# Scores of the last attention on 32-row tiles of four row groups, with unread full-array products in front of side products and value sums

## The chip, the cores and the metric

The kernel runs on one core of a Trainium2 chip. The metric is the device time of one launch in microseconds (us), smaller is better. The core has TensorE (PE in the profile, its weight loads PEld), VectorE (DVE), ScalarE (ACT), GpSimd (POOL) and SyncE (SP), which only starts transfers here. TensorE writes to PSUM, eight banks of 128 partitions by 512 fp32 numbers.

## The reference

Four layers follow each other on an input of 2 x 1024 tokens of width 128. Each normalises `x`, computes an attention `s` and a gate `g`, and adds `s * g`. The change lies in the attention of the last one (`L3_attn`): 16 heads of width 8, causal, on both batch halves.

```python
y = (jnp.einsum('bse,ef->bsf', x, W1) + b1).reshape(B, S, 16, -1).transpose(0, 2, 1, 3)
q, k, v = jnp.split(y, 3, axis=-1)
w = jnp.einsum('bhqd,bhkd->bhqk', q, k) / dk          # dk = 8 ** 0.5
w = jax.nn.softmax(w * mask - 1e10 * (1.0 - mask), axis=-1)   # mask is lower triangular
attn = jnp.einsum('bhqk,bhkd->bhqd', w, v)
return jnp.einsum('bse,ef->bsf', attn.transpose(0, 2, 1, 3).reshape(B, S, E), W2) + b2
```

Its gate is a small quantised product with a low-rank part (`L3_ffn`), worked off beside the first heads.

## The kernel before

Class `Small` does this attention (`kind == 3`; `kind == 1` is the windowed attention of the second layer, which the change leaves as it is). `Lead` (normalisation, gate, values) runs in its first four heads.

*Layout.* Two batch halves of 16 heads make 32 heads `x`. Four heads with the same `n = x // 4` form a quad; head `hh = x % 4` of a quad holds 32 of the 128 partitions: three groups of eight rows with high and low parts of Q and K (the splitting makes up for the fp32r format), and in row 24 of the 32 the row maximum, negated, on Q's side against a one on K's side. Q of a quad lies in `QS[n % 3]` (128 x 1024). K is spread out: `KH[n % 3][hh]` holds the 32 rows of head `hh` and zeros in the other 96, so that a product over all 128 rows gives the scores of one head. ScalarE writes the copies for heads 0 and 2 (`spread`, L2114), GpSimd those for 1 and 3 (`spread_odd`, L1902), each 128 x 512 from `hm`, which holds the projected K.

*Steps.* The order of work is written out: `steps()` goes through head slots `x` of 14 steps `j`. In each step every engine issues what falls due there, in its own queue:
- `row(x, j)`: scores with queries on the partitions (L2007), 12 tiles of at most 512 columns a head (`rparts`). A query block of over 512 keys has two tiles, the first one (`first`) unmasked. VectorE reduces a first tile with one instruction (L2319) into `P2`, and any other with the causal mask added (L2323) into `MM`. After the twelfth one small instruction joins both parts (L2328, event `("both", x)`).
- `col(y, m)`: the scores again with keys on the partitions (L2028), 12 tiles (`cparts`), of the head that is `lag = 63` steps behind (four heads and a half). They contain the maximum through row 24 of Q. ScalarE takes the exp into `ET` (L2135), two buffers.
- `sums`: products of the values with `ET` (L2053), 128-row by 32-column tiles in four column groups, 32 matmuls and then 40, of head `x - 6`, at steps `AV_AT = (0, 4)`. They wait for GpSimd's `cut_off` (L1912), which zeroes the diagonals. ScalarE copies two heads' sums out (`take_out`, L2141) at step 6.
- `misc`: side units at steps 1, 4, 7. `project` makes 512 columns of Q or K of the next quad: three matmuls (L205 to L207), ScalarE's masked copy `hm` (L2102), VectorE's combination (L2235 for Q, L2238 for K). `max` turns the maxima (four transposes, L148) and VectorE adds them into Q (L2251). `give` turns the finished sums back. All use bank 7, one after another.

*Banks and waits.* Row scores go round banks 0 to 2, column scores round 3 to 5. `bank_free` makes TensorE wait until the reader has done with the tile three before. In a step TensorE issues first the column scores, then the row scores, then sums, then a side unit; all queues work strictly in that order. VectorE handles row tile, then side unit. `bc`, `mk` (the mask in bf16, 128 x 512: 384 columns of zeros and the causal block) and the projection weights are set up by `SmallWeights`. SyncE issues nothing in this stage between its loads and the three stores of the result.

The instruction order of TensorE and its waits for a bank:

```python
if m in self.at and 0 <= y < self.NH:
    col(y, self.at[m])
if j in self.at and x < self.NH:
    row(x, self.at[j])
if j in self.AV_AT and 0 <= x - 6 < self.NH:
    sums(x - 6, self.AV_AT.index(j))
if (x, j) in self.misc:
    side(self.misc[x, j])
```

## Time and profile before

| what | value |
|---|---|
| median of 3 runs | 1697.86 us (1697.16 to 1700.54) |
| profiled execution | 1706.63 us |
| its span | 1704.9 us |
| mean granted clock of TensorE | 0.952 |
| last attention | from about 1355 us to the end |

The page gives each engine's busy time and the costliest groups of instructions. The trace answers by stretch: a window of 39.1 us holds one quad of the steady part, in which every head slot has row scores, column scores and sums. The share of busy time of an engine does not say that it sets the pace: the view of waits says who was late for whom, and the view in order of time shows where in a head that happens.

### The profile page before, as it was taken

The page shows a single profiled execution, that of the slowest core. Times are in us where ns is not written, and L with a number is a line of the kernel's source. Part 1 is how long each engine was busy: PE and PEld are TensorE (multiplying, and loading weights), DVE is VectorE, ACT ScalarE, POOL GpSimd, SP SyncE. Part 2 cuts the span into 40 slices and gives each one's busy share as a digit, 9 for nine tenths or more (in the row PEclk, how much of TensorE's full clock was granted, in tenths as well). Part 3 has the DMA queues.
Part 4 walks back from the last instruction along what each step waited for, and adds up shares of the span by engine and source line. Part 5 has one row for each costly group of instructions (what it writes and reads, how often), then busy time and mean ns, then how long its engine had stood idle before and what let it go on. Part 6 is the DMA issues. An engine that isn't in the chain of part 4 may idle for free. (4 is left out here: it accounts for less than half of the span.)

```text
span 1704.9 us, 29946 instructions
## 1 busy us (share of the span) xinstructions
PE 1490.4 (87%) x11248; PEld 1197.3 (70%) x11248; DVE 1260.4 (74%) x2770; ACT 1089.9 (64%) x2122; POOL 857.1 (50%) x798
## 2 busy tenths in 40 slices
PE   6999999999999999899848888845999379998997
PEld 4788887888788887687737676834788256666675
DVE  6999999999999999435461677589433887777772
ACT  4888888888888888455445565632444456666665
POOL 4556576667666666720363744624666632233211
PEclk9999999999999999999779999957999699999999
DMA  3656666656666565300044000040465200000000
GB/s 94 124 103 115 106 120 100 120 108 114 115 108 103 99 105 106 87 1 1 18 137 129 26 2 2 2 133 1 112 148 109 64 1 1 2 2 2 2 2 26
DMA packets 334417, 117.09 MB, mean 69 GB/s; under 512 B 281008, under 2 KB 326096, under 8 KB 334144
## 3 DMA queue, kind: packets, MB, share of 16 engines
q1 hardware_dynamic: 323664, 101.54, 29.2%
q0 software_dynamic: 8496, 12.59, 3.4%
q8 instruction: 89, 1.46, 0.4%
q10 hardware_dynamic: 2112, 1.05, 0.2%
q14 instruction: 56, 0.46, 0.1%
HBM read 37.53 MB, written 10.49 MB: 28 GB/s over the span
## 5 line engine op out<-in xcount | busy, mean ns | idle before, releaser
L2135 ACT ACTIVATE ET_a<-PS 128x256 f32<-128x256 f32 (+2 forms) x512 | 220.5, 499 | 114.8 <-PE PS L2028 72.9
L771 POOL TENSOR_TENSOR dl<-XN,dh 128x1024 f16<-128x1024 f32 x86 | 184.9, 2150 | 155.2 <-DVE D L743 79.7
L205 PE MATMUL PS<-xh,yh 128*128 128x512 f32 x512 | 215.5, 421 | 6.6 <-ACT XNT L608 3.8
L206 PE MATMUL PS<-xl,yh 128*128 128x512 f32 x512 | 204.0, 398 | 0.0
L207 PE MATMUL PS<-xh,yl 128*128 128x512 f32 x512 | 202.8, 396 | 0.0
L608 ACT ACTIVATE G<-PS,nm 128x1024 f32<-128x1024 f32 x128 | 143.0, 1117 | 53.4 <-DVE nm L693 37.9
L608 ACT ACTIVATE XNT<-PS,nm 128x1024 f32<-128x1024 f32 x128 | 143.1, 1118 | 52.3 <-DVE nm L693 41.0
L687 DVE TENSOR_REDUCE nm<-PS 128x1 f32<-128x1024 f32 x128 | 156.6, 1223 | 15.7 <-PE PS L207 13.8
L689 DVE TENSOR_REDUCE nm<-PS 128x1 f32<-128x1024 f32 x128 | 156.0, 1219 | 4.7 <-PE PS L207 1.0
L205 PE MATMUL PS<-dth,xnh 128*128 128x256 f16 x512 | 141.0, 275 | 12.0 <-DVE zl L697 12.0
L2323 DVE CUSTOM_DVE_ANT_0 PS<-PS,mk 128x256 f32<-128x256 f32 (+3 forms) x256 | 128.2, 516 | 30.6 <-PE PS L2007 30.2
L2007 PE MATMUL PS<-KH_a,QS_a 128*128 128x512 f32 (+2 forms) x384 | 132.9, 375 | 13.8 <-DVE top L2323 11.0
L2028 PE MATMUL PS<-QS_a,KH_a 128*128 128x512 f32 (+2 forms) x384 | 136.5, 383 | 6.3 <-DVE QS_a L2251 4.1
L207 PE MATMUL PS<-dth,xnl 128*128 128x256 f16 x512 | 140.1, 274 | 0.0
L206 PE MATMUL PS<-dtl,xnh 128*128 128x256 f16 x512 | 140.0, 274 | 0.0
L771 POOL TENSOR_TENSOR dl<-D,dh 128x1024 f16<-128x1024 f32 x42 | 90.4, 2152 | 76.0 <-DVE XN L743 73.3
L2331 DVE TENSOR_REDUCE XNT<-PS 128x2 f32<-128x448 f32 (+1 forms) x128 | 73.6, 588 | 57.6 <-PE PS L2012 52.4
L205 PEld LDWEIGHTS PS<-xh,yh 128*128 128x128 f32 x512 | 97.2, 190 | 26.5 <-ACT XNT L608 6.3
L207 PEld LDWEIGHTS PS<-xh,yl 128*128 128x128 f32 x512 | 96.8, 189 | 23.9
L1902 POOL TENSOR_SCALAR KH_a<-hm_a,C 128x512 fp32r<-128x512 f32 x32 | 49.7, 1567 | 116.0 <-DVE hm_a L2238 116.0
L2053 PE MATMUL PS<-ET_a,VA 128*32 128x128 f32 (+1 forms) x3712 | 105.4, 257 | 2.9 <-POOL ET_a L1918 2.0
L206 PEld LDWEIGHTS PS<-xl,yh 128*128 128x128 f32 x512 | 97.3, 190 | 11.6
(461 smaller groups left out, 4091.1 us busy)
## 6 DMA issues: line engine op xcount, KB each, us to landing
e_wg<-in_WgT SPq DMA_DIRECT2D x16, 256.0 KB
e_wu<-in_WuT SPq DMA_DIRECT2D x16, 256.0 KB
e_wd<-in_WdT SPq DMA_DIRECT2D x16, 256.0 KB
dth<-dh SPq DMA_TRANSPOSE x128, 3.2
dtl<-dl SPq DMA_TRANSPOSE x128, 3.2
m_x_rows<-m_xs SPq DMA_DIRECT2D x1, 1472.0 KB, 4.9
m_xs<-m_x_rows SPq DMA_DIRECT2D x5, 256.0 KB, 4.8
m_y_rows<-m_xs SPq DMA_DIRECT2D x5, 256.0 KB, 2.3
```

Source lines behind the costliest of these rows:

```text
L205: e.matmul(o, l[0], r[0], start=start, stop=False)
L206: e.matmul(o, l[0], r[1], start=False, stop=False)
L207: return e.matmul(o, l[1], r[0], start=False, stop=stop)
L608: e.activation(self.E[g % 2][:, half, :], self.S[half], ACT.Exp, bias=self.nm[:, half, i:i + 1], scale=1.0, accum_out=self.ss[:, u % 3, ha ...
L687: e.tensor_reduce(self.nm[:, 1, i:i + 1], self.S[1], AX.X, MAX, negate=True).then_inc(*self.top.up((g, 1)))
L689: e.tensor_reduce(self.nm[:, 0, i:i + 1], self.S[0], AX.X, MAX, negate=True).then_inc(*self.top0.up(g))
L771: e.tensor_tensor(self.dl[:, g % 4, :], self.D[g % 3], self.dh[:, g % 4, :], SUB).then_inc(*self.d_low.up(g))
L2007: t = e.matmul(o[:, 0:wd], qs[:, 128 * i:128 * i + 128], kh[:, c0:c0 + wd], start=True, stop=True)
L2028: t = e.matmul(o[:, 0:wd], kh[:, 128 * jj:128 * jj + 128], qs[:, q1 - wd:q1], start=True, stop=True)
L2053: t = e.matmul(k.bank(6)[32 * g:32 * g + 32, c0:c1], w.VA[:, v0:v0 + 32], rhs, start=first, stop=last, skip_group_check=True, tile_positio ...
L2135: e.activation(dst, src, ACT.Exp, scale=self.SC, bias=0.0).then_inc(*self.ex.up(it))
L2323: e.tensor_tensor_reduce(out=o[:, 0:c1 - c0], in0=o[:, 0:c1 - c0], in1=w.mk[:, 512 - (c1 - c0):512], scale=-1.0, scalar=3e38, op0=ADD, op1 ...
```

## The change

- Row and column scores use only the 32 rows of their head: operands `[32 * hh : 32 * hh + 32]` and a tile position in that row group. `KH` with its zeros and all copies into it go; K of a quad lies in `KA[n % 3]` (as Q in `QA`, of which `QS` is a view), written directly by VectorE's combination.
- Odd tiles (`j % 2`) use the row group two further, from swapped copies `KZ` and `QZ` (partitions 0 to 63 and 64 to 127 exchanged). SyncE makes them: for each projection of 512 columns two transfers of 64 partitions, for each `max` unit two of two partitions (rows 24 of the heads). A swap waits for the fourth one before it. Row scores of the first quad do not use them.
- TensorE issues the row scores of a step ahead of the column scores; with `lag = 70` (five heads) the four matmuls of two steps lie in four different row groups.
- `whole(o)`: a bf16 product over the full array into the bank that the next unit overwrites, never read. It stands in front of each `project` (not of the first quad), `max` and `give`, 512 columns wide, and twice, 256 wide, in front of the first part of `sums`.
- `sums` move to steps 4 and 10, part 0 waits for the first `cut_off` only; `take_out` to step 12; side units to steps 0, 1, 5, 8.
- Row tiles of the split query blocks change order, the second tile starts its minimum from the first one's in `P2`, and the joining instruction goes.

```diff
...
-        self.KH = [[sb(f"KH{n}_{i}", [128, 1024], F32R) for i in range(4)] for n in range(3)]
+        if kind == 3:
+            self.KA, self.KZ, self.QZ = [sb(n, [128, 3, 1024], F32R) for n in ("KA", "KZ", "QZ")]
+        else:
+            self.KH = [[sb(f"KH{n}_{i}", [128, 1024], F32R) for i in range(4)] for n in range(3)]
...
             self.rparts, self.cparts = [], []
+            firsts, seconds = [], []
             for i in range(8):
                 w_ = 128 * (i + 1)
                 cut = 0 if w_ <= 512 else (384 if w_ == 640 else 512)
-                self.rparts += [(i, 0, cut, True)] * (cut > 0) + [(i, cut, w_, False)]
+                if cut == 0:
+                    self.rparts += [(i, 0, w_, False)]
+                else:
+                    firsts.append((i, 0, cut, True))
+                    seconds.append((i, cut, w_, False))
                 lo = 128 * i
                 w_ = 1024 - lo
                 cut = 1024 if w_ <= 512 else lo + (384 if w_ == 640 else 512)
                 self.cparts += [(i, lo, cut)] + [(i, cut, 1024)] * (cut < 1024)
+            self.rparts += [firsts[0], firsts[1], seconds[0], firsts[2], seconds[1], firsts[3], seconds[2], seconds[3]]
         else:
             self.rparts, self.cparts = list(range(4)), list(range(4))
         self.nr, self.nc_ = len(self.rparts), len(self.cparts)
         self.avs = [self.av_of(x) for x in range(NH)]
         na = max(len(p_) for p_ in self.avs[0])
-        self.AV_AT = (0, 4) if kind == 3 else (11, 12)
-        self.lag = 63 if kind == 3 else 70
+        self.AV_AT = (4, 10) if kind == 3 else (11, 12)
+        self.lag = 70
...
                 continue
             if hh == 0 and 1 <= n <= self.NQ:
-                m += [("max", n - 1, c) for c in range(2)]
-            if n + 1 < self.NQ and hh in (1, 2):
-                m += [("project", n + 1, w_, hh - 1) for w_ in (1, 0)]
+                m += [(1, ("max", n - 1, 0)), (5, ("max", n - 1, 1))]
+            if n + 1 < self.NQ:
+                m += {1: [(1, ("project", n + 1, 1, 0)), (8, ("project", n + 1, 0, 0))], 2: [(0, ("project", n + 1, 1, 1))],
+                      3: [(1, ("project", n + 1, 0, 1))]}.get(hh, [])
             if x - 7 >= 1 and (x - 7) % 2 and x - 7 < NH:
-                m += [("give", x - 7)]
+                m += [(8, ("give", x - 7))]
...
+                m += [(2, ("sum", (x - 34) // 2))]
+            for j, what in m:
+                self.misc[x, j] = what
...
+        self.swaps = [u for u in use if u[0] in ("project", "max")]
+        self.swapped = [k.sig(f"a_swapped{i}", grid(self.swaps[i::4], range(2)), 16) for i in range(4)] if kind == 3 else None
...
             self.moe.sp_rows(e, q)
+        if self.kind == 1:
+            return
+        for m, u in enumerate(self.swaps):
+            n, ck = u[1], u[-1]
+            cs = slice(512 * ck, 512 * ck + 512)
+            if m >= 4:
+                self.swap_landed(q, self.swaps[m - 4])
+            q.wait_ge(self.mi, u)
+            if u[0] == "project":
+                src, dst = (self.KA, self.KZ) if u[2] else (self.QA, self.QZ)
+                parts = slice(0, 64), slice(64, 128)
+                if n >= 3:
+                    q.wait_ge(self.col, ("col", 4 * (n - 3) + 3, self.nc_ - 1))
+            else:
+                src, dst = self.QA, self.QZ
+                parts = slice(24, 57, 32), slice(88, 121, 32)
+                self.swap_landed(q, ("project", n, 0, ck))
+            for i in range(2):
+                e.dma_start(f(dst[parts[1 - i], n % 3, cs]), f(src[parts[i], n % 3, cs])).then_inc(*self.swapped[m % 4].up((u, i)))
+
+    def swap_landed(self, q, u):
+
+        q.wait_ge(self.swapped[self.swaps.index(u) % 4], (u, 1))
...
         else:
-            for ck in range(2):
-                self.spread_odd(e, q, ("project", 0, 1, ck))
             for x in range(self.NH + 5):
-                n, hh = divmod(x, 4)
-                if hh in (1, 2) and n + 1 < self.NQ:
-                    self.spread_odd(e, q, ("project", n + 1, 1, hh - 1))
...
                 self.gate.pool_step(e, q, x)
 
...
-
-        _, n, w_, ck = u
-        hn = self.hm[self.hm_n[u] % len(self.hm)]
-        q.wait_ge(self.mi, u)
-        for hh in (1, 3):
-            self.k_free(q, n, hh)
-            e.tensor_scalar(self.KH[n % 3][hh][:, 512 * ck:512 * ck + 512], f(hn), self.k.cst("block")[:, hh:hh + 1], None, MUL).then_inc(
-                *self.k_dve.up(("k", n, ck, hh)))
...
+        def whole(o):
+
+            q.wait_ge(w.ready, "mask")
+            e.matmul(o, w.mk[:, 384:512], w.mk[:, 0:o.shape[-1]], start=True, stop=True)
+
         def project(u, o):
             _, n, w_, ck = u
             b, qd = divmod(n, 4)
+            if self.kind == 3 and n:
+                whole(o)
...
-            q.wait_ge(self.top, ("both", 4 * n + 3) if self.kind == 3 else ("row", 4 * n + 3, self.nr - 1))
+            q.wait_ge(self.top, ("row", 4 * n + 3, self.nr - 1))
             o = k.bank(self.side_of[u])
+            if self.kind == 3:
+                whole(o)
...
-                q.wait_ge(self.k_act if hh % 2 == 0 else self.k_dve, ("k", n, (c0 + max(c1 - c0, 256) - 1) // 512, hh))
+                q.wait_ge(self.mi, ("project", n, 1, (c0 + max(c1 - c0, 256) - 1) // 512))
                 q.wait_ge(self.mi, ("project", n, 0, i // 4))
             elif j == 0:
...
-                t = e.matmul(o[:, 0:wd], qs[:, 128 * i:128 * i + 128], kh[:, c0:c0 + wd], start=True, stop=True)
+                if n and j % 2:
+                    self.swap_landed(q, ("project", n, 1, (c0 + wd - 1) // 512))
+                    self.swap_landed(q, ("project", n, 0, i // 4))
+                    hh, qs, kh = (hh + 2) % 4, self.QZ[:, n % 3, :], self.KZ[:, n % 3, :]
+                r = slice(32 * hh, 32 * hh + 32)
+                t = e.matmul(o[:, 0:wd], qs[r, 128 * i:128 * i + 128], kh[r, c0:c0 + wd], start=True, stop=True, tile_position=(32 * hh, 0))
...
             if self.kind == 3:
                 jj, q0, q1 = self.cparts[j]
                 wd = max(q1 - q0, 256)
-                t = e.matmul(o[:, 0:wd], kh[:, 128 * jj:128 * jj + 128], qs[:, q1 - wd:q1], start=True, stop=True)
+                if j % 2:
+                    for c in range(2):
+                        self.swap_landed(q, ("project", n, 1, c))
+                        self.swap_landed(q, ("max", n, c))
+                    hh, qs, kh = (hh + 2) % 4, self.QZ[:, n % 3, :], self.KZ[:, n % 3, :]
+                r = slice(32 * hh, 32 * hh + 32)
+                t = e.matmul(o[:, 0:wd], kh[r, 128 * jj:128 * jj + 128], qs[r, q1 - wd:q1], start=True, stop=True, tile_position=(32 * hh, 0))
...
             per, et = self.avs[x], self.ET[x % 2]
+            q.wait_ge(self.cut, (x, part if self.kind == 3 else 1))
...
                 q.wait_ge(w.ready, "va0")
                 if self.kind == 3:
                     q.wait_ge(p.vals, 3)
                 if x >= 2 and hh % 2 == 0:
                     q.wait_ge(self.out, x - 1)
+                if self.kind == 3:
+                    for i in range(2):
+                        whole(k.bank(6)[:, 256 * (hh % 2):256 * (hh % 2) + 256])
             for j in self.av_parts[part]:
                 for g in range(4):
...
             if self.lead:
                 self.lead.pe_at(e, q, x, j)
             y, m = divmod(14 * x + j - self.lag, 14)
+            if self.kind == 3 and j in self.at and x < self.NH:
+                row(x, self.at[j])
             if m in self.at and 0 <= y < self.NH:
                 col(y, self.at[m])
-            if j in self.at and x < self.NH:
+            if self.kind == 1 and j in self.at and x < self.NH:
                 row(x, self.at[j])
             if j in self.AV_AT and 0 <= x - 6 < self.NH:
                 sums(x - 6, self.AV_AT.index(j))
...
         def project(u, o):
             high(u, o)
-            spread(u)
+            if self.kind == 1:
+                spread(u)
...
             if w_:
                 q.wait_ge(self.mi, u)
-                for hh in heads:
...
-                    to, own = self.KH[n % 3][hh][:, 512 * ck:512 * ck + 512], k.cst("block")[:, hh:hh + 1]
-                    if self.kind == 3:
-                        e.activation(to, f(hn), ACT.Copy, scale=own).then_inc(*self.k_act.up(("k", n, ck, hh)))
-                    else:
-                        e.activation(to[r, :], f(hn[r, :]), ACT.Copy).then_inc(*self.k_act.up(("k", n, ck, hh)))
...
                 high(self.first[m], k.bank(m))
-            spread(self.first[0], (0,))
             high(self.first[3], k.bank(3))
-            spread(self.first[2], (0,))
             for c in range(2):
                 self.lead.take(e, q, c, k.bank(4 + c))
-            for m in (0, 2):
-                spread(self.first[m], (2,))
             self.lead.act_rest(e, q)
...
-            if j == (6 if self.kind == 3 else 13) and 0 <= x - 6 < self.NH and x % 2:
+            if j == (12 if self.kind == 3 else 13) and 0 <= x - 6 < self.NH and x % 2:
...
             q.wait_ge(self.mi_act, u)
-            if w_ == 0:
+            if w_ == 0 or self.kind == 3:
                 if n >= 3:
                     q.wait_ge(self.col, ("col", 4 * (n - 3) + 3, self.nc_ - 1))
-                e.scalar_tensor_tensor(out=self.QS[n % 3][:, cs], in0=o, scalar=self.bq[:, w_, qd:qd + 1], in1=f(hn), op0=ADD,
+                to = self.KA[:, n % 3, cs] if w_ else self.QS[n % 3][:, cs]
+                e.scalar_tensor_tensor(out=to, in0=o, scalar=self.bq[:, w_, qd:qd + 1], in1=f(hn), op0=ADD,
...
                         q.wait_ge(w.ready, "mask")
+                    least = 3e38
+                    if c0:
+                        least = self.P2[:, n % 2, i - 4, hh:hh + 1]
+                        q.wait_ge(self.top, ("row", x, self.rparts.index((i, 0, c0, True))))
                     e.tensor_tensor_reduce(out=o[:, 0:c1 - c0], in0=o[:, 0:c1 - c0], in1=w.mk[:, 512 - (c1 - c0):512], scale=-1.0,
-                                           scalar=3e38, op0=ADD, op1=MIN, accum_out=dst).then_inc(*self.top.up(it))
-                if j == self.nr - 1:
-                    m4 = M[:, 4:8, col].rearrange("p i c -> p (i c)")
-                    q.wait_ge(self.top, it)
-                    e.tensor_tensor(m4, m4, self.P2[:, n % 2, :, hh], MIN).then_inc(*self.top.up(("both", x)))
+                                           scalar=least, op0=ADD, op1=MIN, accum_out=dst).then_inc(*self.top.up(it))
             else:
                 lo, hi = 0 if j == 0 else 32, 256 if j == 3 else 224
                 e.tensor_reduce(M[:, 2 * j:2 * j + 2, col].rearrange("p i c -> p (i c)"), o.rearrange("p (j c) -> p j c", j=2)[:, :, lo:hi], AX.X, MAX,
...
```

## Rows read from the trace of the kernel before

**Rows 1.** The page, part 1: engine, busy us, share of the span, instructions.

```profile
PE 1490.4 (87%) x11248; PEld 1197.3 (70%) x11248; DVE 1260.4 (74%) x2770; ACT 1089.9 (64%) x2122; POOL 857.1 (50%) x798
```

**Rows 2.** Windows, a quad and the end: PE, PEld, DVE, ACT, POOL, clock, DMA.

```profile
1480.10:1519.20 39.10, 35.48 (x413) 26.46 (x412) 29.95 (x97) 26.20 (x59) 11.13 (x12) 1.00 0.01 2
1658.70:1704.90 46.20, 36.73 (x552) 27.57 (x544) 12.79 (x27) 25.15 (x60) 6.37 (x10) 0.98 0.08 24
```

**Rows 3.** Waits in that quad: who for whom, us in total, times, longest.

```profile
ACT ET_a L2135 <- PE PS L2028: 10.4, 10, 3.0
DVE PS L2323 <- PE PS L2007: 4.5, 6, 0.9
DVE QS_a L2235 <- ACT hm_a L2102: 2.6, 2, 1.3
DVE hm_a L2238 <- ACT hm_a L2102: 2.2, 2, 1.1
```

**Rows 4.** TensorE in order of time: start, us to the last end, what, count.

```profile
1488.85 0.28 PE L2007 MATMUL PS<-KH_a,QS_a 128*128 128x256 f32 x1
1489.06 1.08 PE L2053 MATMUL PS<-ET_a,VA 128*32 128x128 f32 x32
1490.07 0.50 PE L2028 MATMUL PS<-QS_a,KH_a 128*128 128x512 f32 x1
1490.41 0.28 PE L2007 MATMUL PS<-KH_a,QS_a 128*128 128x256 f32 x1
1490.53 0.39 PE L205 MATMUL PS<-q_xh,W4h 128*128 128x512 f32 x1
1490.76 0.40 PE L206 MATMUL PS<-q_xl,W4h 128*128 128x512 f32 x1
```

**Rows 5.** VectorE in order of time, same head; idle time before in brackets.

```profile
1490.73 0.43 DVE L2323 CUSTOM_DVE_ANT_0 PS<-PS,mk 128x256 f32<-128x256 f32 x1 [0.82 <-PE PS L2007]
1492.31 0.75 DVE L2238 SCALAR_TENSOR_TENSOR hm_a<-PS,bq,hm_a 128x512 fp32r<-128x512 f32 x1 [1.10 <-ACT hm_a L2102]
```

**Rows 6.** Head 3 as a window; VectorE's groups in the quad: busy us, mean ns.

```profile
1382.30:1388.30 6.00, 3.84 (x17) 2.50 (x17) 5.99 (x21) 5.10 (x8) 0.00 (x0) 1.00 0.00 0
...
L2238 DVE SCALAR_TENSOR_TENSOR hm_a<-PS,bq,hm_a 128x512 fp32r<-128x512 f32 x2 | 1.5, 750 | 2.2 <-ACT hm_a L2102 2.2
L2251 DVE TENSOR_TENSOR QS_a<-QS_a,PS 128x512 fp32r<-128x512 f32 x2 | 1.4, 688 | 0.5 <-PE PS L148 0.5
L2328 DVE TENSOR_TENSOR top<-top,P_a 128x4 f32<-128x4 f32 x4 | 0.7, 168 | 0.1
```

**Rows 7.** Weight loads in order of time: start, us.

```profile
1502.35 0.19 PEld L2028 LDWEIGHTS PS<-QS_a,KH_a 128*128 128x128 f32 x1 [0.19 <-ACT ET_a L2135]
1502.46 0.19 PEld L2007 LDWEIGHTS PS<-KH_a,QS_a 128*128 128x128 f32 x1
```

**Rows 8.** Window before a fall of the clock; eight matmuls at half and full clock.

```profile
1443.50:1446.90 3.40, 1.93 (x8) 1.08 (x7) 2.13 (x7) 2.86 (x8) 2.77 (x4) 1.00 0.00 0
...
1389.30 1.92 PE L3304 MATMUL PS<-early,XNT 128*128 128x128 f32 x8
1395.54 1.05 PE L3304 MATMUL PS<-early,XNT 128*128 128x128 f32 x8
```

**Rows 9.** One line's instructions, bf16 over the full array: ns min/median/max.

```profile
L2009 PE MATMUL PS<-mk,identb x128: 376/390/650, 867.1 to 1085.4; 128*128 128x512 bf16 x128
```

**Rows 10.** Transfers: queue, count, KB, us to landing.

```profile
C<-in_consts SPq DMA_DIRECT2D x1, 128.0 KB, 2.2
```

**Rows 11.** Heads 0 to 4 as a window; K copies in the quad: busy us, mean ns.

```profile
1355.00:1399.20 44.20, 34.44 (x159) 25.27 (x160) 37.38 (x118) 25.59 (x48) 17.19 (x13) 0.88 0.00 1
...
L2114 ACT ACTIVATE KH_a<-hm_a,C 128x512 fp32r<-128x512 f32 x4 | 2.7, 714 | 1.6 <-DVE hm_a L2238 1.6
...
L1902 POOL TENSOR_SCALAR KH_a<-hm_a,C 128x512 fp32r<-128x512 f32 x4 | 6.2, 1566 | 16.2 <-DVE hm_a L2238 16.2
```

**Rows 12.** The joining instruction over all heads: ns min/median/max, first and last start.

```profile
L2328 DVE TENSOR_TENSOR top<-top,P_a x32: 167/168/1249, 1363.8 to 1658.7; 128x4 f32<-128x4 f32 x32
```

35 lines of the change are left out of this document (15 added, 20 removed).

## The prediction

> **What bounds the kernel now.** I read the page first: TensorE is busy 87% of the span and VectorE 74% [rows 1]. Those are averages over four layers, so the next view is the busy time by stretch. The change touches only the last attention, which runs from about 1355 us to the end. Its steady part repeats every four heads ("a quad"), because projections, maxima and returned outputs come in a pattern of four. One quad takes 39.1 us: TensorE is busy 35.5, VectorE 29.95, ScalarE 26.2, GpSimd 11.1, at full clock [rows 2]. So TensorE looks like the bound at 91%, but the reader should not stop there. The wait view of the same quad shows that TensorE and VectorE wait for each other in turn. VectorE is idle 9.15 us. It waits 4.5 us for row scores and 4.8 us for the ScalarE half of a projection (2.6 + 2.2); ScalarE waits 10.4 us for column scores [rows 3]. The value sums are why row scores are late: 32 matmuls from 1489.06 keep TensorE from scores until 1490.07 [rows 4]. VectorE, which has at most three banks of row scores in store, sits idle 0.82 us, gets one tile, and then waits 1.10 us for the projection that was queued behind the sums as well [rows 5]. What a VectorE head costs without such waits is shown by head 3, where no column scores or sums run yet: 6.0 us, VectorE busy 5.99 [rows 6]. Four of these plus the side work come to the 29.95 us. So the question is how much of 9.15 us of VectorE idle time per quad goes when TensorE is relieved. The distance from the first to the last joining of maxima is 294.9 us for 31 heads [rows 7].
>
> **The change, part by part.**
> *Scores on 32-row tiles.* A head has 24 score matmuls with 4,736 columns for rows and as many for columns. Back to back, 512 columns are 0.23 us apart and 256 columns 0.12 us [rows 4], that is 0.45 ns a column, so 9,472 columns cost 4.3 us per head. After the change neighbours in the queue lie in four different row groups, and can run side by side. The trace has no row-tiled stream, so I bound it. The worst case is no overlap: 4.3 us, and perhaps some 0.1 us more each, if a load cannot run ahead. The value sums are the nearest rows: their four column groups overlap, 40 matmuls of 128 columns in little over 1.2 us, 0.03 us each. The best case takes that, 24 x 0.03 = 0.8 us. Between them stands the weight port: loads of 128 columns start 0.11 us apart at the densest [rows 8], and all 24 loads stay, so 24 x 0.11 = 2.6 us. I take 2.6, since these rows show the same load shape: 1.7 us per head saved on TensorE.
> The page "TensorE: Matmul & The Clock Gate" of the Trainium skill, Part 3, gives a speedup of 3.07 for four row tiles of 512 columns; by it the scores would cost an estimated 1.4 us. No row here shows it.
> *Tile forms that alternate.* From a full-array score to the column-tiled sums the distance is 0.21 us in place of 0.12 (1488.85 to 1489.06), and back to a score there is another 0.11 us (0.34 in place of 0.23, 1490.07 to 1490.41) [rows 4]. So a change of form costs about 0.1 us. Today a head has four; after it the two side units per head add two each, and the unread products in front of the sums one: five more, 0.5 us of TensorE. The Trainium skill's "TensorEngine Tiling (Array Packing)", Key Properties, says that a change of tiling mode drains the engine. The trace agrees with its 0.1 us; it speaks against this change, but at that price does not undo it.
> *Unread bf16 products.* One of 512 columns precedes each side unit from head 1 on (28 projections, 16 maxima, 16 returns), two of 256 precede each head's sums. A bf16 matmul of 512 columns lasts 0.39 us [rows 9], the same as its fp32r kin, so I price it by the spacing, 0.23 us: 8 x 0.23 + 8 x 0.12 = 2.8 us per quad, 0.7 us per head. Ends: 0.04 us each if they slip under others, 0.39 if nothing overlaps. They hold up their side unit by 0.23 us.
> *TensorE sum.* -1.7 + 0.5 + 0.7 = -0.5 us of work per head, while 3.6 us of a quad were idle. That is small. What matters more is the order:
> *Order.* Sums move from steps 0 and 4 to steps 4 and 10; side units move off them (1, 5, 8, 0 in place of 1, 4, 7). Today a head with two projections pays both waits at both places [rows 5]. After it, the row score goes first in its step, with no column score (0.34 us at 1490.07) in front, and the sums start with about 1.5 us of row scores in store (a 384, a 512 and a 384 tile at step 4). They need 0.1 + 0.24 + 1.0 + 0.1 + 0.4 until the next row tile is there, 1.85 us; at step 10 about 0.1 + 1.25 + 0.1 + 0.4 = 1.85 against 1.5. So about 0.35 us remains at each, 0.7 per head, 2.8 per quad; but part of it may be caught up by overlap, and I take 2.5 against the 4.5 of today. Projections: chain of 0.1 + 0.23 + 0.7 + 0.17 on TensorE and 0.78 + about 0.2 of ScalarE, 2.2 us, against 1.25 to 1.4 us in store; about 0.95 us wait for each of four: 3.8 in place of 4.8. Together -3.0 us per quad.
> *Copies of K dropped.* ScalarE loses 0.715 us four times in a quad, GpSimd 1.57 us four times, two of each by two heads [rows 10]; VectorE writes K at once, as it does Q, at the same 0.75 us [rows 6]. Neither engine was the bound. What they hid: the exps queued behind the copies get free 0.7 us earlier, and the next projection does not wait for a buffer; I price it at nothing in the steady part. At the start, heads 0 to 4 wait for these copies among others; VectorE is busy 37.4 of 44.2 us there [rows 10], and of the 6.8 idle I take 2.
> *Maxima.* The joining instruction goes: 168 ns [rows 6], with the wait for its own input ahead of it an estimated 0.26 us per head. Four reductions per head now read the first part's minimum from a [128,1] operand in place of a constant: the nearest pair is an add with such an operand (751 ns) and one without (688) [rows 6], so 0 to 0.06 each; I take 0.03, 0.1 per head. Net -0.15 us per head, -0.6 per quad. The wait that is added is for a result at least one instruction old.
> *Swapped copies.* SyncE issues 96 transfers between SBUF partitions: 64 of 128 KB, 32 of 4 KB. SBUF to SBUF is not in the trace; from HBM 128 KB lands in 2.2 us [rows 11]. The DMA queues are nearly empty in this stage and SyncE has nothing else before the end. The tightest user is the second column tile of a quad's first head, ten steps (about 6 us) after the second maxima unit: 1 us of transposes, 0.7 of add, 2.5 of transfer, so it fits by 1 to 2 us. Nothing, then; each us beyond would be paid once a quad, 7 us in all.
> *Lag.* Column scores follow rows by five whole heads, not four and a half. Half a head more is left for the end, where ScalarE is the pace-setter; but there the first column head hides the last maxima chain, for which all stood still. The end now takes 46.2 us from the last joining [rows 2]; I leave it at that, +/-4.
> *Sum.* 27 heads run in the steady form, 6.75 quads: 6.75 x (3.0 + 0.6) = 24 us, minus some 4 us that ScalarE's in-order waits give back (take-outs at step 12 now sit right behind sums), plus 2 at the start: 22 us. The profiled run took 1706.6 us (span 1704.9); 22 off is 1684.6. The median of the plain runs lies 8.8 below the profiled one, so **1676 us**.
>
> **Rivals.**
> *A, the forecast*: 1660 to 1691. Chance 0.50.
> *B, VectorE at its floor*: the row scores overlap freely and all 4.5 us of row waits go with 1 us of the work: 5.5 to 6.5 a quad, 37 to 44 us, plus 4 at the start: 1650 to 1659. For it: VectorE's own load is only 76%. Against: the sums stay a block of 1.0 and 1.2 us. 0.15.
> *C, no relief*: the row groups do not overlap, or the swaps land late, and added products and form changes (+1.2 us per head) eat what the order brings: 1692 to 1701. 0.18 in all, half of it within 0.2%.
> *D, the clock falls (slower)*: the array has less to do between sums. Just before the clock fell at 1446.9 TensorE had been busy 1.93 of 3.4 us [rows 12], and quarter-array scores may keep it down much more often. At 1.2 GHz eight matmuls of 128 columns take 1.92 us in place of 1.05 [rows 12]; so a head's sums cost 2.3 us more and its side work about 1, 3 us less what VectorE's slack takes. 27 heads wholly at 1.2 GHz would lose 81 us; the gain of 22 is gone at 27% of the stage, and at half of it the time is 1676 + 40 = 1716. For it: a quarter of the rows in 24 of a head's matmuls, and denser packing that leaves TensorE idle for longer between. Against: sums and side units are spread more evenly, and full-array products come with each. 0.17.
>
> **How the numbers follow.** The likeliest case gives 1676. B reaches to 1650, D beyond 1710; below 1649 lies about 0.06 and above 1710 about 0.12, so the range is 1649 to 1710. About 0.2% (3.4 us) is what a measurement of this kernel tells from no change. Faster: A, B and half of C, 0.74; same 0.09; slower 0.17.
>
> **What would show it.** In the profile after: a quad of about 35.5 us, VectorE busy over 80% of it; row-score waits of VectorE near 2.5 us a quad; score matmuls 0.11 us apart or less when the queue is full; clock full in all but a few stretches; no wait on a transfer. The prediction is wrong if quarter-array scores are spaced 0.2 us or more, if the clock falls in over a quarter of the stage, or if column scores wait for swaps.

## The result and the profile after

The changed kernel is slower: a median of 1709.86 us (1706.89 to 1717.95, 5 runs) against 1697.16 us (1695.11 to 1700.54) for the kernel before in the same comparison, ratio 1.0085 with a 95% interval of 1.0067 to 1.0104. I had forecast 1676 us and gave "slower" a chance of 0.17. The time lies at the upper edge of the range, the direction is wrong.

A slip first: the prediction numbers its groups of rows differently from the section that shows them. Its 1 to 6 and 9 are right; its 7 is group 12 there, 8 is 7, 10 is 11, 11 is 10, and 12 is 8. From here on the numbers are those of that section.

The page of the changed kernel, part 1, and the clock lines of part 2, of before and then of the changed kernel. VectorE has 32 instructions less, the joining ones; against [rows 1] the busy shares hardly move.

```profile
PE 1499.9 (88%) x11372; PEld 1162.7 (68%) x11372; DVE 1263.1 (74%) x2738; ACT 1075.3 (63%) x2090; POOL 808.2 (47%) x766
...
PEclk9999999999999999999779999957999699999999
PEclk9999999999999999999789999867998768897889
```

What moved is in the last quarter of the clock line. The digits 7, 6, 8 stand where the clock is at 1.2 GHz for part of a slice and at 2.4 GHz for the rest. The mean granted clock fell from 0.952 to 0.928.

To place the loss I cut the stage by heads. Every head has one row reduction of 128 columns on VectorE; the distance between two of them is the time of a head. In the profiled runs (spans 1704.9 and 1706.5 us; the layers ahead of this stage took 11 us longer in the run of before, so only the stage is compared):

| stretch | before, us (at 1.2 GHz) | after, us (at 1.2 GHz) |
|---|---|---|
| head 0 to head 5 | 43.9 (10.2) | 39.8 (13.7) |
| head 5 to head 31 | 251.8 (6.8) | 264.6 (85.3) |
| head 31 to the end | 53.9 (2.0) | 58.3 (8.4) |
| sum | 349.7 | 362.8 |

The difference of 13.1 us fits the medians' 12.7. Heads 5 to 31 are 26 heads. The best quad of the changed kernel, heads 15 to 18, took 9.6, 8.9, 9.7 and 9.7 us, 37.9 in all, 1.2 less than the 39.1 of before. Its first head is not clean: it holds 3.4 us at 1.2 GHz (heads 7, 11, 19, 23 and 27, which have the same work, hold 3.4 to 4.6), and VectorE's longest wait of the quad ended there. The same wait in the run e6 below, at full clock (VectorE in order of time, changed kernel and then e6):

```profile
1499.89 0.76 DVE L2363 CUSTOM_DVE_ANT_0 PS<-PS,mk,P_a 128x512 f32<-128x512 f32 x1 [1.98 <-PE PS L2041]
...
1498.02 0.76 DVE L2363 CUSTOM_DVE_ANT_0 PS<-PS,mk,P_a 128x512 f32<-128x512 f32 x1 [0.58 <-PE PS L2041]
```

So the quad would take an estimated 37.9 - 1.4 = 36.5 us at full clock. Heads that ran at 1.2 GHz for 90% or more of their time took 11.3, 13.8 and 13.9 us, where heads in the same places of a quad took 9.7, 9.7 and 8.9 at full clock. The last two of the 26 have no side work left and take 7.7 and 8.2 us. All heads like the best quad would be 6 x 37.9 + 15.9 = 243.3 us, and at full clock an estimated 6 x 36.5 + 15.9 = 234.9; they took 264.6. So the 85.3 us at 1.2 GHz cost at least 21 us, by the estimate 30. The same sum for before is 6 x 39.1 + 15.7 = 250.3, 1.5 less than its 251.8. At full clock the change was thus worth at least 7 us, by the estimate 15, and the clock took two to three times that.

A window at full clock (34.1 us), the one behind it, at half clock, and the last window before each of two falls. Columns as in [rows 2]: PE, PEld, DVE, ACT, POOL, clock, DMA.

```profile
1500.10:1534.20 34.10, 29.95 (x381) 17.44 (x380) 28.56 (x87) 23.49 (x52) 4.85 (x8) 1.00 0.15 33
1534.20:1551.30 17.10, 16.49 (x157) 10.03 (x155) 10.20 (x31) 6.70 (x16) 1.50 (x3) 0.50 0.01 2
...
1530.80:1534.20 3.40, 2.91 (x37) 1.33 (x26) 3.40 (x10) 2.46 (x7) 0.40 (x1) 1.00 0.35 77
1561.50:1564.90 3.40, 1.89 (x12) 0.91 (x11) 2.44 (x10) 2.69 (x6) 0.25 (x1) 1.00 0.35 77
```

At half clock VectorE was busy 60% of the time (10.20 of 17.10) and TensorE 96%: there TensorE is the bound, and the slack of VectorE that I had counted on is no cover. Before the fall at 1564.9 TensorE was busy 1.89 of 3.4 us, much as in [rows 8]; but before the one at 1534.2 it was busy 2.91 of 3.4, with 37 matmuls. Busy time alone does not foretell a fall.

VectorE's waits in the full-clock window (who for whom, us in total, times, longest), the counterpart of [rows 3]. The 2.0 of the first line is the wait that ended at 1499.89, ahead of the window and at 1.2 GHz, so that only 0.2 + 0.8 = 1.0 us of waits for row scores lies inside:

```profile
DVE PS L2363 <- PE PS L2041: 2.2, 2, 2.0
DVE KA_a L2273 <- ACT hm_a L2148: 2.1, 2, 1.1
DVE QS_a L2273 <- ACT hm_a L2148: 1.8, 2, 1.0
DVE P_a L2355 <- PE PS L2041: 0.8, 1, 0.8
DVE QS_a L2287 <- PE PS L148: 0.4, 1, 0.4
```

Each of four projections still holds VectorE for 1 us. No view names a swapped copy as what an engine waited for. The trace has no landing times for these transfers, but between 1441 and 1640 us TensorE never sat idle before a column score (L2068), and no weight load of a row score had more than 0.4 us of idle time that the view leaves unexplained. So the transfers are hidden, as assumed.

TensorE in order of time in the same window (start, us, what, count):

```profile
1503.59 0.49 PE L2041 MATMUL PS<-KZ_a,QZ_a 32*128 32x512 f32 x1
1503.60 0.38 PE L2068 MATMUL PS<-QZ_a,KZ_a 32*128 32x256 f32 x1
1504.02 0.39 PE L1947 MATMUL PS<-mk 128*128 128x512 bf16 x1
1504.24 0.60 PE L148 MATMUL PS<-C,top 128*128 128x128 f32 x4
1504.77 0.38 PE L2041 MATMUL PS<-KA_a,QS_a 32*128 32x256 f32 x1
1504.78 0.44 PE L2068 MATMUL PS<-QS_a,KA_a 32*128 32x384 f32 x1
1504.78 0.50 PE L2041 MATMUL PS<-KZ_a,QZ_a 32*128 32x512 f32 x1
1504.78 0.38 PE L2068 MATMUL PS<-QZ_a,KZ_a 32*128 32x256 f32 x1
1505.00 0.28 PE L2041 MATMUL PS<-KA_a,QS_a 32*128 32x256 f32 x1
```

The row groups do overlap: four scores of 256, 384, 512 and 256 columns start within 0.01 us, and the next one 0.23 us later. Over the full array their 1,408 columns would need 0.63 us at the 0.45 ns a column of [rows 4]. On the other side, the pair at 1503.6 is followed by the product 0.42 us later, and the transposes (four of them, 0.22 us behind the product) by the next scores 0.53 us later; in the run e10 below, with full-array scores, the same step takes 0.35 (1505.55 to 1505.90). It is not the bf16 format that costs this: in e10 the unread product starts 0.24 us behind a full-array score of 512 columns, and the transposes 0.23 behind the product (1505.08, 1505.32, 1505.55).

### The profile page after: what moved, and what is told of

Read it like the earlier page. It is cut to its first block, busy times and chain, and to the rows that moved or that the text cites. A ratio compares the mean times of both kernels' runs of the same rounds, so it can differ in the third digit from the quotient of the medians.

```text
span 1706.5 us, 30348 instructions
## 1 busy us (share of the span) xinstructions
PE 1499.9 (88%) x11372; PEld 1162.7 (68%) x11372; DVE 1263.1 (74%) x2738; ACT 1075.3 (63%) x2090; POOL 808.2 (47%) x766
## 4 chain that ended last, share of the span: by engine, by line
PE 25%; DVE 12%; ACT 4%; POOL 4%; issue 3%; DMA 2%; ACTq 0%; DVEq 0%; POOLq 0%
PE PS L2096 5%; PE PS L2041 3%; PE PS L148 2%; DVE PS L2363 2%; DVE P_a L2355 2%; PE PS L2894 2%; PE PS L2878 2%; ACT hm_a L2148 2%; PE PS L2895 2%; PE PS L1947 2%; PE PS L2074 1%; PE PS L2068 1%; DVE e_junk L3059 1%; ACT ET_a L2178 1%; POOL m_x_rows L1450 1%
## 5 line engine op out<-in xcount | busy, mean ns | idle before, releaser
L2178 ACT ACTIVATE ET_a<-PS 128x256 f32<-128x256 f32 (+2 forms) x512 | 228.1, 493 | 150.4 <-PE PS L2068 110.3
L1930 POOL TENSOR_SCALAR_AFFINE_SELECT ET_a<-ET_a 128x512 f32<-128x512 f32 x64 | 40.6, 635 | 287.1 <-ACT ET_a L2178 287.1
L608 ACT ACTIVATE G<-PS,nm 128x1024 f32<-128x1024 f32 x128 | 142.9, 1117 | 53.2 <-DVE nm L693 37.8
L2096 PE MATMUL PS<-ET_a,VA 128*32 128x128 f32 (+1 forms) x3712 | 120.7, 281 | 2.5 <-POOL ET_a L1936 2.3
L2096 PEld LDWEIGHTS PS<-ET_a,VA 128*32 128x32 f32 x3712 | 95.5, 120 | 24.0 <-issue 14.8
L2041 PE MATMUL PS<-KA_a,QS_a 32*128 32x256 f32 (+2 forms) x216 | 81.0, 426 | 20.3 <-DVE top L2363 12.3
L2355 DVE TENSOR_REDUCE P_a<-PS 128x1 f32<-128x512 f32 (+1 forms) x128 | 82.0, 651 | 16.2 <-PE PS L2041 15.5
```

The lines of the kernel that those rows point to most:

```text
L608: e.activation(self.E[g % 2][:, half, :], self.S[half], ACT.Exp, bias=self.nm[:, half, i:i + 1], scale=1.0, accum_out=self.ss[:, u % 3, ha ...
L2041: t = e.matmul(o[:, 0:wd], qs[r, 128 * i:128 * i + 128], kh[r, c0:c0 + wd], start=True, stop=True, tile_position=(32 * hh, 0))
L2096: t = e.matmul(k.bank(6)[32 * g:32 * g + 32, c0:c1], w.VA[:, v0:v0 + 32], rhs, start=first, stop=last, skip_group_check=True, tile_positio ...
L2178: e.activation(dst, src, ACT.Exp, scale=self.SC, bias=0.0).then_inc(*self.ex.up(it))
L2355: e.tensor_reduce(dst, o[:, 0:c1 - c0], AX.X, MAX, negate=True).then_inc(*self.top.up(it))
```

## Experiments

Each run was timed beside the kernel before on the same chip, and three chips were used (before took 1709.7 us beside e1 to e4, 1696.5 beside e5 to e8 and 1709.1 beside e9 to e11), so the ratios are to be compared, not the times. "Quad" is one at full clock; the values in brackets hold 3.4 us at 1.2 GHz, since these runs have no quad free of it, and e2 has none with so little. "End" is from head 31's reduction. The profiled execution of e2 was the slowest of its five (1750.0 us against a median of 1737.4, mean clock 0.889 against 0.900), so its row shows somewhat more time at 1.2 GHz than is usual for it.

| kernel | ratio | quad, us | head 5 to 31, us (at 1.2 GHz) | end, us |
|---|---|---|---|---|
| before | 1 | 39.1 | 251.8 (6.8) | 53.9 |
| changed | 1.0085 | (37.9) | 264.6 (85.3) | 58.3 |
| changed once more (e8) | 1.0100 | (37.9) | 264.8 (85.3) | 63.7 |
| e1 constant start and joining back | 1.0083 | (38.0) | 255.0 (58.0) | 60.0 |
| e2 without unread products | 1.0146 | | 285.3 (182.2) | 56.4 |
| e3 one more product per row score | 1.0504 | 52.1 | 333.3 (0.0) | 61.4 |
| e4 before + new order | 0.9944 | 38.0 | 247.9 (10.2) | 53.2 |
| e9 before + late combining | 0.9937 | 38.0 | 241.5 (0.0) | 53.9 |
| e5 e4 + late combining | 0.9811 | 34.7 | 223.2 (0.0) | 53.2 |
| e7 e5, sums in four parts | 0.9876 | 36.8 | 234.0 (0.0) | 52.7 |
| e10 e5 + unread products | 0.9913 | 36.8 | 236.0 (0.0) | 55.8 |
| e6 changed + late combining | 0.9989 | 34.6 | 234.9 (37.5) | 56.1 |
| e11 e6 without unread products | 1.0069 | (34.7) | 254.4 (122.9) | 66.2 |

**e1_join: the maxima.** The changed kernel with the joining instruction back and a constant start value:

```diff
-                    if c0:
-                        least = self.P2[:, n % 2, i - 4, hh:hh + 1]
-                        q.wait_ge(self.top, ("row", x, self.rparts.index((i, 0, c0, True))))
...
+                if j == self.nr - 1:
+                    m4 = M[:, 4:8, col].rearrange("p i c -> p (i c)")
+                    q.wait_ge(self.top, it)
+                    e.tensor_tensor(m4, m4, self.P2[:, n % 2, :, hh], MIN).then_inc(*self.top.up(("both", x)))
```

> The changed kernel with one thing undone: the joining instruction over both parts of the maxima is back, and the second tiles start from a constant again. Theory 1 (the new reduction costs more than the joining one: 0.06 us for each of four and a stall of 0.17 us between the last two, against 0.19 us for the joining one, net 0.24 us a head): VectorE's 32 heads get 8 us cheaper; where VectorE paces them, 4 to 8 us come off, about 1703 us. Rival (TensorE at half clock paces the stage, VectorE has slack): under 2 us of difference.

Measured 1.0083 (1.0059 to 1.0106) against 1.0085 and 1.0100 (1.0077 to 1.0122) for the changed kernel. The best quad, with the same 3.4 us at 1.2 GHz in it, is the same to 0.1 us, and so is VectorE's busy time in it (30.6 us, changed 30.5). So the form of the maxima makes no difference that shows in the time, in either direction (the rival held), though the reductions themselves differ. The same form (128 x 512 and 128 x 256) of VectorE's groups from 1600 to 1640 us in the changed kernel, reading `P_a` (us busy, mean ns), and then in e1 with a constant:

```profile
L2363 DVE CUSTOM_DVE_ANT_0 PS<-PS,mk,P_a 128x256 f32<-128x256 f32 x8 | 3.9, 482 | 0.0
L2363 DVE CUSTOM_DVE_ANT_0 PS<-PS,mk,P_a 128x512 f32<-128x512 f32 x5 | 3.8, 758 | 4.1 <-PE PS L2041 4.1
```

```profile
L2360 DVE CUSTOM_DVE_ANT_0 PS<-PS,mk 128x512 f32<-128x512 f32 x8 | 5.7, 719 | 2.8 <-PE PS L2041 2.8
L2360 DVE CUSTOM_DVE_ANT_0 PS<-PS,mk 128x256 f32<-128x256 f32 x12 | 5.2, 432 | 0.0
```

The operand costs 39 to 50 ns a reduction, four a head, and the reductions with a constant start are longer beside them too (455 in place of 432 ns for 256 columns, 333 in place of 287 for 128). Together that is about as much as the joining instruction that the change saves, 220 ns in e1.

**e2_no_whole and e3_more_whole: what holds the clock.** Both change only products that nothing reads. e2 leaves them out of the changed kernel. e3 adds one of 512 columns ahead of each row score from the second quad on:

```diff
+                if n:
+                    whole(o)
                 r = slice(32 * hh, 32 * hh + 32)
                 t = e.matmul(o[:, 0:wd], qs[r,
```

> The changed kernel without the unread products of the last attention (124 matmuls gone, the result is the same). Theory 1 (the clock decides, and these products hold it up for part of the time): the clock is at 1.2 GHz for clearly more than the 85 of 265 us of heads 5 to 31, half of them or more, and the time goes up by 5 to 30 us. Rival (they are mere extra work, 19 us of TensorE by their spacing of 0.23 and 0.12 us, and do not move the clock): about the same clock, and 5 to 10 us faster than the changed kernel.

> The changed kernel with one more unread 512-column product, in front of every row score from the second quad on (12 per head, 336 in all, 2.6 us of TensorE a head at 0.22 us each). Theory 1 (the clock decides): it stays at 2.4 GHz in nearly all of heads 5 to 31, heads go to the 9.4 us that the changed kernel shows at full clock if the products fit into idle time of TensorE, and the time falls to 1685 to 1695 us; if they do not fit, it stays near 1705. Rival (order and VectorE decide, not the clock): TensorE only gets more work, 1715 to 1740 us.

e2 is slower than the changed kernel, as the theory had it: 1.0146 (1.0121 to 1.0170). e3 is slower than either of its forecasts, 1798.4 us, ratio 1.0504, where 1685 to 1740 was expected: the clock came out as the theory said, the price of the products did not. Windows of one length, 1400 to 1640 us, of e2, of the changed kernel, of e3 and of the kernel with the new order and full-array scores (e4, below), in this order:

```profile
1400.00:1640.00 240.00, 216.22 (x2151) 126.99 (x2149) 170.24 (x506) 133.42 (x291) 26.77 (x42) 0.70 0.12 27
```

```profile
1400.00:1640.00 240.00, 217.22 (x2543) 127.45 (x2535) 178.92 (x539) 143.34 (x317) 30.22 (x48) 0.86 0.12 26
```

```profile
1400.00:1640.00 240.00, 230.87 (x2070) 116.42 (x2107) 152.56 (x426) 126.28 (x250) 22.95 (x36) 1.00 0.10 22
```

```profile
1400.00:1640.00 240.00, 215.52 (x2477) 165.33 (x2481) 191.47 (x598) 166.04 (x358) 68.52 (x73) 0.98 0.01 2
```

TensorE is busy 216, 217 and 216 us in e2, the changed kernel and e4, and is granted 0.70, 0.86 and 0.98. What differs is how much of the work covers the whole array. With fewer full-array products the clock falls more, with more it does not fall at all (in e3 TensorE is also busy longer, 231 us). The closest pair is e6 and e10 below: same order, same products, same late combining, TensorE on row tiles in one and on the full array in the other, and 37.5 against 0.0 us at 1.2 GHz between heads 5 and 31. Rival D's cause is therefore shown: it is the row-tiled form of the scores that lets the clock down, and the products hold up only a part. The direct and swapped copies and the order of the row tiles come with that form in every pair and were not tried alone (the maxima were, in e1). What it is in the row tiles, that each fills a quarter of the array or that four run at once and the queue is done sooner, is not shown either. That the products are mere extra work, to be dropped for a gain, is refuted: the kernel without them is slower than with them, though they cost time where the clock is full (e10). e3 shows the price of a full cure. TensorE of e3 in order of time:

```profile
1504.28 0.39 PE L1947 MATMUL PS<-mk 128*128 128x512 bf16 x1
1504.60 0.38 PE L2043 MATMUL PS<-KA_a,QS_a 32*128 32x256 f32 x1
1504.60 0.50 PE L2070 MATMUL PS<-QS_a,KA_a 32*128 32x512 f32 x1
1505.03 0.39 PE L1947 MATMUL PS<-mk 128*128 128x512 bf16 x1
1505.35 0.38 PE L2043 MATMUL PS<-KZ_a,QZ_a 32*128 32x256 f32 x1
```

A round of one product and two scores takes 0.75 us: product to score 0.32, score to product 0.43. The same three spaced as in [rows 4] would be 0.23 + 0.12 + 0.23 = 0.58, without any overlap. So with a change of form at each step the row tiles lose more than they bring.

**e4_order_only: the order without the tiles.** The kernel before, with full-array scores, the copies `KH` and the joining instruction, and of the change only the order: sums at (4, 10), row score first, side units at the new steps, take-out at step 12, lag 70. The row tiles of a head keep their old order.

```diff
...
-        self.AV_AT = (0, 4) if kind == 3 else (11, 12)
-        self.lag = 63 if kind == 3 else 70
+        self.AV_AT = (4, 10) if kind == 3 else (11, 12)
+        self.lag = 70
...
+            if self.kind == 3 and j in self.at and x < self.NH:
+                row(x, self.at[j])
             if m in self.at and 0 <= y < self.NH:
                 col(y, self.at[m])
...
```

> The kernel before with only the new order: row scores first in a step, lag of five heads, sums at steps 4 and 10, side units at 0, 1, 5, 8, take-out at step 12. Full-array scores with K copies and the joining instruction stay, no unread products. Theory 1 (the order was worth about 2 to 3 us a quad on VectorE's waits, as forecast): 1675 to 1690 us, clock full. Rival (the order brings nothing without relieved TensorE, and half a head more at the end costs up to 4 us): 1697 to 1702 us.

Measured 0.9944 (0.9925 to 0.9963), a full-clock quad of 38.0 us, 1.1 less than before where 2 to 3 were expected. Of the estimated 2.6 us (39.1 to 36.5) that the whole change is worth in a quad at full clock, 1.1 thus come from the order alone. The other 1.5, by the same estimate, come with row tiles, direct copies and maxima, net of the products; with late combining (e5, e6) nothing is left of them, and they cost the clock and the end.

**e5, e6 and e9: VectorE's wait for ScalarE.** What was left at 1 us for each projection is a wait for ScalarE's half. VectorE stands in its queue in front of the combination until ScalarE's masked copy is there, with row tiles ready behind it. In these runs the combination is taken two steps later in VectorE's queue (and ScalarE's copy of K three steps later where there is one):

```diff
...
-            if (x, j) in self.misc:
+            if self.kind == 3 and self.misc.get((x, j - 2), ("",))[0] == "project":
+                side(self.misc[x, j - 2])
+            if (x, j) in self.misc and (self.kind == 1 or self.misc[x, j][0] != "project"):
                 side(self.misc[x, j])
```

e5 puts this on e4, e6 on the changed kernel, e9 on the kernel before with its old order.

> The kernel before with the new order (as in the run with the order alone, 0.994 of the time of before), and in it VectorE combines a projection two steps after its place, ScalarE copies K three steps after it. Theory 1 (what paces heads at full clock is VectorE waiting about 1 us for each of four projections a quad): those 4 us go from a quad of 38 us, 20 to 27 us in all over 27 heads, ratio 0.978 to 0.984. Rival (TensorE's full-array scores bind, so the wait only moves to row scores): ratio 0.99 to 0.995.

> The changed kernel with VectorE's combination of a projection two steps after its place. Theory 1 (row-tiled scores leave TensorE room, but the clock falls in a third of the stage): the same 4 us a quad at full clock, 0.6 us less per quad than the full-array variant can show, but the clock falls as often; ratio to before 0.990 to 1.000. Rival (with the projection waits gone the row-tiled form shows its worth): below the full-array variant, 0.97 or less.

> The kernel before with one edit: VectorE combines a projection two steps later, and ScalarE copies its part of K three steps later; the old order of sums and side units stays. Theory (what paces VectorE is mostly its in-order wait for ScalarE's half, 4.8 us a quad): this edit alone brings most of what the run with new order and late combining brought: a full-clock quad of 35 to 36.5 us in place of 39.1, ratio 0.982 to 0.989. Rival (late combining pays only together with the new order, since the sums stand right in front of the side units here and the row waits take over): a quad of 37.5 to 38.5, ratio 0.990 to 0.997.

e5 is the fastest kernel of the study: 1664.71 us, ratio 0.9811 (0.9796 to 0.9826), within its theory's range. e6 comes to 0.9989 (0.9971 to 1.0006), e9 to 0.9937 (0.9922 to 0.9953). At full clock the quads of e5 and e6 are 34.7 and 34.6 us: both forms of the scores run equally fast, and the 22.9 us between their profiled runs lie in heads 0 to 5 (50.2 us, 41.0 of them at 1.2 GHz, against 41.8 with 10.2), in heads 5 to 31 (234.9 with 37.5 against 223.2 with none) and in the end (56.1 against 53.2).

Why does the order bring 1.1 us a quad alone, late combining 1.1 alone, and both 4.4? VectorE's longest waits in the 120 us from 1480, of e4, then e9, then e5:

```profile
DVE PS L2326 <- PE PS L2008: 11.0, 16, 1.9
DVE hm_a L2241 <- ACT hm_a L2105: 4.8, 7, 0.9
DVE QS_a L2238 <- ACT hm_a L2105: 4.6, 6, 1.0
DVE P_a L2322 <- PE PS L2008: 1.9, 4, 0.6
```

```profile
DVE PS L2326 <- PE PS L2007: 22.3, 30, 1.0
```

```profile
DVE PS L2329 <- PE PS L2008: 11.6, 25, 0.8
DVE QS_a L2257 <- PE PS L148: 0.7, 4, 0.2
```

Counted over whole quads at full clock, from head to head, VectorE has these times, in us a quad (the changed kernel's is its best quad, with 3.4 us at 1.2 GHz):

| kernel | busy | waits for row scores | waits for ScalarE's half |
|---|---|---|---|
| before | 30.0 | 3.6 | 4.8 |
| e4 new order | 30.7 | 4.1 | 2.9 |
| e9 late combining | 30.2 | 6.7 | 0 |
| e5 both | 30.9 | 3.3 | 0 |
| changed | 30.5 | 3.0 | 3.7 |
| e6 changed + late combining | 30.5 | 3.4 | 0 |

In e9 the projection waits are gone, but the row waits grow from 3.6 to 6.7 us: VectorE empties its three banks earlier and then stands before the sums. The new order alone (e4) does not shorten the row waits; what it takes off is 1.9 us of the waits for ScalarE. Only both edits end the projection waits and keep the row waits at 3.3. My theory for e9, that late combining alone brings most, fell; its rival held.

**e7_order_late_four: smaller blocks of sums.** e5 with the sums in four parts:

```diff
...
-        self.AV_AT = (4, 10) if kind == 3 else (11, 12)
+        self.AV_AT = (2, 5, 8, 11) if kind == 3 else (11, 12)
...
```

> As the full-array variant with late projections, and the value sums of a head in four parts (16, 16, 16, 24 matmuls) at steps 2, 5, 8, 11 in place of two of 32 and 40. Theory 1 (blocks of 1.0 and 1.25 us of sums starve VectorE once each, about 0.7 us a head): 2 us more off a quad, 10 to 14 us in all, against two more changes of tile form each way (0.4 us a head of TensorE). Rival (TensorE binds here, so the form changes cost what they last): 0 to 12 us slower than the variant with two parts.

Measured 0.9876 (0.9861 to 0.9891), the quad 36.8 us in place of 34.7; the rival held. Two more blocks a head are four more changes of form, 16 a quad: at most 2.1 / 16 = 0.13 us for each if nothing else changed. In e5 TensorE is busy 117 of 120 us, with little slack to hide them.

**e10 and e11: what products and tiles do at full clock.** e10 is e5 plus the unread products at the places of the change. e11 is e6 without them.

```diff
...
+        def whole(o):
+            q.wait_ge(w.ready, "mask")
+            e.matmul(o, w.mk[:, 384:512], w.mk[:, 0:o.shape[-1]], start=True, stop=True)
...
+            if self.kind == 3 and n:
+                whole(o)
...
```

> The new order with late combining, full-array scores, plus the unread bf16 products at the same places as in the changed kernel. It prices the products by themselves at full clock. Theory 1 (TensorE has slack now: it was busy 117 of 120 us by the trace's rows, but those overlap): 0.23 us for each of 8 and 0.12 for each of 8 come to 2.8 us of TensorE a quad, of which some half appears: a quad of 35.5 to 36.5, ratio 0.986 to 0.992. Theory 2 (TensorE is the bound at 34.7): all 2.8 appear: a quad of 37.5, ratio 0.993 to 0.997. Theory 3 (hidden): a quad of 34.7 to 35.2, ratio 0.981 to 0.985. The clock should stay full in all three.

> The changed kernel with late combining and without the unread products: row-tiled scores stand alone. Theory (quarter-array scores alone do not keep the clock up): far more than the 37.5 us at 1.2 GHz of heads 5 to 31, at least 100 of some 260 us, ratio 1.005 to 1.025. Rival (the tighter packing that late combining gives is enough to hold the clock, and the products only cost): under 40 us at half clock, a full-clock quad of 33 to 34, ratio 0.985 to 0.995.

e10: 0.9913 (0.9897 to 0.9929), a quad of 36.8 us and a full clock. So the products cost 2.1 us a quad, between the first two theories, of the 2.8 of matmul time that they add; the ratio lies in the range of the first. e6, which has the same products and the row tiles, has 34.6: row tiles, with the direct copies, the maxima and the order of the row tiles that come with them, bring 2.2 us a quad back. In e11 the clean heads take 8.3, 8.5 and 8.5 us where e6 has 8.9, 8.8 and 9.1, so the products cost 0.5 us a head there too; but 122.9 of 254.4 us run at 1.2 GHz, ratio 1.0069 (1.0041 to 1.0096), as the theory had it. The windows from 1480 to 1600 of e5, e6, e10 and e11:

```profile
1480.00:1600.00 120.00, 117.01 (x1438) 91.11 (x1436) 106.48 (x334) 89.20 (x198) 36.16 (x40) 1.00 0.01 2
```

```profile
1480.00:1600.00 120.00, 106.99 (x1441) 65.07 (x1456) 103.40 (x316) 83.13 (x185) 17.13 (x27) 0.97 0.15 33
```

```profile
1480.00:1600.00 120.00, 117.95 (x1407) 89.63 (x1395) 101.57 (x314) 87.01 (x190) 37.98 (x40) 1.00 0.01 2
```

```profile
1480.00:1600.00 120.00, 110.49 (x1295) 67.21 (x1295) 95.82 (x290) 74.82 (x168) 15.93 (x25) 0.80 0.13 28
```

In e6 TensorE is busy 89% and VectorE 86%; in e5 98% and 89%. So the tiles do relieve TensorE, yet VectorE of e6 waits no less for row scores than that of e5:

```profile
DVE PS L2363 <- PE PS L2041: 8.4, 18, 1.4
DVE P_a L2355 <- PE PS L2041: 6.2, 9, 1.2
```

That is 14.6 us against the 11.6 above, in 120; but e6 has 6.8 us at 1.2 GHz in this window, and in quads at full clock it is 3.4 against 3.3. The likely reason that the relief does not shorten these waits, argued from the order of the queue and not tried, is that products and changes of form stand in front of rows that are due. What the tiles save, the products take back, and without the products the clock takes more.

**e8_changed_again** is the changed kernel unedited, timed on the chip of e5 to e7.

> The changed kernel itself, unedited, on the chip of the other three, so that the variants are compared with it there. Both theories: the ratio of 1.0085 to before again, 1.006 to 1.011, with the clock at 1.2 GHz for 70 to 110 us of heads 5 to 31.

1.0100 (1.0077 to 1.0122), which agrees with the first comparison. Between heads 5 and 31 its profile repeats the first one (264.8 us, 85.3 at 1.2 GHz); its end took 63.7 us with 24.1 at 1.2 GHz in place of 58.3 with 8.4. In both profiles the falls of the steady part are the same, so they belong to the kernel; those in the end vary.

## Why the prediction was wrong, step by step

**The likeliest case.** It fell at the chance of rival D. D's mechanism was written down and is what happened: I priced it at 3 us a head at 1.2 GHz with the break-even at 27% of the stage. The three heads almost wholly at half clock took 1.6, 4.1 and 5.0 us more than heads in the same places of a quad at full clock, and 32% of the time from head 5 to 31 was at half clock. The step that failed is that the sum had no term for the clock. What stood in for one was the argument against D, "sums and side units are spread more evenly, and full-array products come with each", and the check "clock full in all but a few stretches". Before has 24 full-array scores in a head, after none; the 16 products of a quad do not stand in for them (e2, e3, e6 and e10). The term would have been at least +21 us, by the estimate +30. I had a row that should have raised the chance: in [rows 8] the kernel before itself loses the clock, with TensorE busy 1.93 of 3.4 us.

**Row waits, 4.5 to 2.5 a quad, and projection waits, 4.8 to 3.8.** The 4.5 was misread. It holds a wait of 0.84 us that lay ahead of the window of [rows 3]; with it the waits add up to more than VectorE's idle 9.15 us. From head to head before has 3.6. In the changed kernel the best quad has 3.0, of which 2.0 is the one wait at 1.2 GHz, so an estimated 1.6 at full clock: the size of the gain, 2.0, was right. Its reason was not: by e4 the order, which the prediction called what matters more, leaves the row waits at 4.1 when it comes alone, so the relief came with the row tiles or what goes along with them. The projection waits are 3.7, as forecast; e4 puts that down to the order. VectorE's work did not get shorter (30.5 us a quad, before 30.0), where the maxima were to take 0.6 off. So the quad gained an estimated 2.6 us at full clock where I had 3.6, and 1.2 as measured.

**Scores, -1.7 us a head.** The bound that I took, one weight load each 0.11 us, does not hold: four scores with different weights start within 0.01 us of each other. What the tiles are worth in time at full clock is 2.2 us a quad, 0.55 a head, by e10 against e6.

**Form changes, 0.1 us each.** Too low for row tiles. e3 has 0.32 us from a 512-column product to a score and 0.43 from a pair of scores to a product, where full-array neighbours of the same size are 0.23 apart: 0.1 and 0.2 us more, and the second holds what the longer of two scores needs. The sentence "it speaks against this change, but at that price does not undo it" stands on this term. The Trainium skill ("TensorEngine Tiling (Array Packing)", Key Properties) says that a change of mode drains the engine; the trace agrees, in that these starts are 0.1 and 0.2 us later.

**Unread products, +0.7 us a head on TensorE.** Nearly right on the path where TensorE is the bound: 0.5 us a head (e10, e11).

**Maxima, -0.15 us a head.** The operand costs 0.04 to 0.05 us, not 0.03, in four reductions, and their neighbours are longer too, which brings the term to nothing; e1 shows no difference in time.

**Copies of K dropped, swaps at nothing, start -2.** Right for the swaps: nobody waits for them. Heads 0 to 5 took 4.1 us less; e4 without direct copies took 39.1 us there, so this, too, may be the order, and the runs of the start scatter (39.1 to 50.2) with their clock.

**End, left at +/-4.** It grew by 4.4 us, and by 9.8 in e8. e4, with the new lag and full-array scores, has 53.2: the lag costs nothing. e10 adds 2.6 us with the products alone. The rest of the growth goes with the row tiles and the clock (8.4 and 24.1 us at 1.2 GHz).

**Sum.** With the best quad as it is, the steady part gained 7 us and the clock cost 21, 1.5 of which before had paid as well; the end cost 4.4, the start gave 4.1: -7 + 21.3 - 1.5 + 4.4 - 4.1 = 13.1 us, the difference of the table. With the estimated quad of 36.5 it is 15 gained and 30 lost. So of the 24 us forecast for the steady part some 15 were there at full clock, and the clock took twice as much.

**What stays open.** Why the falls come where they do: windows with TensorE busy 1.89 and 2.91 of 3.4 us both stood before one, a window with 3.17 (1516.8 to 1520.2) before none, and e6 spent nine tenths of heads 1 to 6 at 1.2 GHz and later quads at full clock with the same attention work. Which property of the row tiles lets the clock down is open, too. Which share of the end's growth is clock and which is form changes was not told apart.

## What to carry to other kernels

In this kernel row tiles that fill a quarter of the array were packed four abreast and yet lowered TensorE's clock: read the granted clock beside the busy time, and price such a change at half clock before counting its columns. When two engines wait for each other in turn, removing one wait feeds the other; here two edits of 1.1 us each made 4.4 together. An in-order engine that stands before another engine's half of a result, with finished input behind it, can take the combination later: two steps later ended that wait here, for 1.1 us a quad by itself and 3.3 behind the new order. And a wait view can count a wait that lies ahead of its window: check its sum against the idle time before building on it.
